# Four normalisation tails reordered: centre and gamma ahead of the root, epsilon as its bias, scale behind it

## The reference

```python
def _layernorm(x, eps=1e-05):
    return (x - mean(x)) / sqrt(var(x) + eps)

h = max(_layernorm(x), 0)                       # layer 0
y = relu((x_sum_of_neighbours(h) + (1 + eps0) * h) @ W1.T + b1) @ W2.T + b2
x = x + ((y - mu(y)) * rsqrt(var(y) + 1e-5) * gamma + beta)

h = max(_layernorm(x), 0)                       # layer 1, attention over the edges, 8 heads
y = h + attention(h) @ Wo
z = (y - mu) * rsqrt(var + 1e-5) * ln1_g + ln1_b
y = z + relu(z @ W1 + b1) @ W2 + b2
x = x + ((y - mu) * rsqrt(var + 1e-5) * ln2_g + ln2_b)

h = max(_layernorm(x), 0)                       # layer 2, edge weights, message width 256
g = relu((messages(h) @ W1 + b1, normalised over 128 features) * gamma + beta)
x = x + where(valid, relu(g @ W2 + b2), 0)

h = max(_layernorm(x), 0)                       # layer 3, mean over neighbours
x = x + relu(mean_of_neighbours(h) @ W_l.T + b_l + h @ W_r.T)
```

## Time and profile before

| | |
|---|---|
| median of three runs | 1396.78 us |
| profiled execution | 1398.88 us |
| its span | 1397.1 us |
| mean granted TensorE clock | 0.948 |
| TensorE busy | 1214.6 us (87%) |
| VectorE busy | 647.5 us (46%) |
| ScalarE busy | 427.1 us (31%) |
| GpSimd busy | 138.5 us (10%) |

### The profile page before, as it was taken

The page is one execution under the profiler, slowest core; times in us unless marked ns, Lnnn a source line. Parts: engine busy times, 40 slices in busy tenths (PEclk is TensorE's granted clock), DMA queues, the critical chain, the costliest instruction groups (busy, mean ns, idle before and its releaser), DMA issues.

```text
span 1397.1 us, 18693 instructions
## 1 busy us (share of the span) xinstructions
PE 1214.6 (87%) x6185; PEld 745.0 (53%) x6185; DVE 647.5 (46%) x1642; ACT 427.1 (31%) x708; POOL 138.5 (10%) x113
## 2 busy tenths in 40 slices
PE   1477777778899998998999999999987999899998
PEld 0244444444465544555777777775446655655543
DVE  6766666666500485003666666665557200540033
ACT  2401122222000434104565555653335301650000
POOL 0000000000145224000000000002326000200000
PEclk9978897878899999999999999999999999999999
DMA  4012344444677610100000000006000032000010
GB/s 138 0 27 56 88 129 137 125 137 132 210 283 249 213 61 30 41 20 1 1 2 1 2 2 1 2 2 247 0 0 31 1 135 79 1 30 0 0 38 36
DMA packets 41609, 93.85 MB, mean 67 GB/s; under 512 B 5113, under 2 KB 9920, under 8 KB 41526
## 3 DMA queue, kind: packets, MB, share of 16 engines
q1 hardware_dynamic: 41526, 92.74, 20.8%
HBM read 51.76 MB, written 34.56 MB: 62 GB/s over the span
## 4 chain that ended last, share of the span: by engine, by line
PE 76%; DVE 11%; issue 6%; ACT 3%; DVEq 2%; DMA 1%; SPq 0%; POOLq 0%; POOL 0%; ACTq 0%
PE PS L403 14%; PE PS L615 6%; PE PS L437 6%; PE PS L598 6%; PE PS L730 6%; PE PS L572 6%; PE PS L479 5%; PE PS L764 5%; PE PS L543 5%; PE PS L701 3%; PE PS L709 3%; PE PS L452 2%; PE PS L533 2%; DVE R L1000 2%; DVE stats L861 2%
## 5 line engine op out<-in xcount | busy, mean ns | idle before, releaser
L403 PE MATMUL PS<-HT,R 125*128 (+1 forms) x988 | 241.7, 379 | 96.9 <-DVE HT L885 43.8
L885 DVE TENSOR_SCALAR HT<-BC,K 125x626 f16 (+1 forms) x494 | 193.0, 443 | 115.1 <-PE PS L403 77.2
L403 PEld LDWEIGHTS PS<-HT,R 125*128 x988 | 139.0, 158 | 199.4 <-issue 177.3
L989 DVE CUSTOM_DVE_ANT_0 HT<-PS,CD 128x1250 f32<-128x1250 f32 (+1 forms) x80 | 116.4, 1454 | 54.2 <-issue 54.2
L1153 ACT COPY HT<-PS 128x626 f32<-128x626 f32 x80 | 54.6, 683 | 253.4 <-PE PS L403 251.2
L598 PE MATMUL PS<-K,HT 128*128 128x128 f32 (+2 forms) x800 | 111.7, 278 | 15.8 <-DVE R L1000 15.0
L1247 ACT ACTIVATE HT<-HT,soft 128x1250 f32<-128x1250 f32 (+1 forms) x80 | 107.1, 1338 | 19.9 <-DVE soft L992 12.6
L598 PEld LDWEIGHTS PS<-K,HT 128*128 128x128 f32 (+2 forms) x800 | 83.4, 140 | 43.5 <-DVE R L1000 24.2
L1227 ACT COPY R<-PS 128x512 f32<-128x512 f32 (+1 forms) x120 | 64.8, 574 | 120.1 <-PE PS L598 118.2
L572 PE MATMUL PS<-R 64*128 64x512 f32 (+3 forms) x480 | 94.8, 526 | 4.8 <-DVE soft L989 3.1
L615 PE MATMUL PS<-R 128*64 128x128 f32 (+2 forms) x1600 | 94.2, 273 | 0.0
(11 more groups left out here) (192 smaller groups left out, 1381.5 us busy)
## 6 DMA issues: line engine op xcount, KB each, us to landing
edge_parts<-HT SPq DMA_DIRECT2D x80, 234.4 KB
X<-edge_parts SPq DMA_DIRECT2D x15, 625.0 KB, 5.7
R<-edge_parts SPq DMA_DIRECT2D x15, 625.0 KB, 5.8
CD<-HT SPq DMA_DIRECT2D x160, 39.1 KB
edge_counts<-CD SPq DMA_DIRECT2D x10, 625.0 KB, 5.9
CD<-edge_sums SPq DMA_DIRECT2D x1, 6250.0 KB, 21.6
CD<-edge_counts SPq DMA_DIRECT2D x1, 6250.0 KB, 17.8
X<-in_x SPq DMA_DIRECT2D x2, 2304.0 KB
```

The lines of the kernel that those rows point to most:

```text
L403: i = mm(bank(b0 + h, PIECE), stat, hot[:, h * PIECE:(h + 1) * PIECE], start=first, stop=True, skip_group_check=True)
L885: return ve.tensor_scalar(slot, iota[0:EC, :], K1[0:EC, K_BASE + w:K_BASE + w + 1], col, ALU.add, ALU.is_equal)
L989: ve.tensor_tensor_reduce(Pb[s][a][0:n], PS[0:n, a * N:(a + 1) * N], cd[0:n, t, :], 1.0, -3e38, ALU.add, ALU.max, soft[0:n, s, a:a + 1]).t ...
```

## The change

In the four tails the order of the normalisation is another. Before: scale and shift on ScalarE, (y x scale - mean x scale), then gamma on VectorE. After: (y - mean) x gamma in one scalar_tensor_tensor on VectorE, right behind the variance and ahead of the root's use; then y x scale on ScalarE, as a Copy with a per-partition scale and no bias. GpSimd's beta addition waits for ScalarE's scaling (`_z`) and no longer for a gamma product (`_zg`). Epsilon is no longer added by VectorE: the root takes it as a per-partition bias from a constant. Since `spread_of` and `root` are shared, that also holds for the three norms of x behind the first tail, the third tail and the loop `l2b`.

```diff
+            ve.memset(gate[:, 1:2], LN_EPS)
 ...
             def spread_of(y, n, slot, name, s, m):
                 link(ve.bn_stats(s[0:n, 0, :], y))
-                link(ve.bn_aggr(m[0:n, slot, :], s[0:n, 0, :]))
-                ve.tensor_scalar(m[0:n, slot, 1:2], m[0:n, slot, 1:2], LN_EPS, None, ALU.add).then_inc(sem(name + "_var"), 1)
+                ve.bn_aggr(m[0:n, slot, :], s[0:n, 0, :]).then_inc(sem(name + "_var"), 1)
 ...
-            def spread_of_y(name, t, w=D, buf=ybuf):
-                spread_of(y_of(t, w, buf), rows(t), t % 4, name, stats, mv)
-            def scale_of_y(name, t):
-                scale_of(rows(t), t % 4, name, t, mv, rs)
-            def scaled(st, t, gamma, w=D, buf=ybuf):
-                n = rows(t)
-                dve.wait_ge(sem(st + "_z"), t + 1)
-                ve.tensor_tensor(y_of(t, w, buf), y_of(t, w, buf), gamma[0:n], ALU.mult).then_inc(sem(st + "_zg"), 1)
+            def spread_of_y(st, t, gamma, w=D, buf=ybuf):
+                n, y = rows(t), y_of(t, w, buf)
+                spread_of(y, n, t % 4, st + "_yn", stats, mv)
+                dve.wait_ge(sem(st + "_yn_var"), t + 1)
+                ve.scalar_tensor_tensor(y, y, mv[0:n, t % 4, 0:1], gamma[0:n], ALU.subtract, ALU.mult)
+            def scale_of_y(st, t):
+                n = rows(t)
+                dve.wait_ge(sem(st + "_yn_std"), t + 1)
+                ve.reciprocal(rs[0:n, t % 4, 0:1], rs[0:n, t % 4, 0:1]).then_inc(sem(st + "_yn"), 1)
 ...
-                    spread_of_y("l0_yn", t)
+                    spread_of_y("l0", t, bc0[:, 1, :])
                 if 1 <= t <= T:
-                    scale_of_y("l0_yn", t - 1)
-                if 2 <= t < T + 2:
-                    scaled("l0", t - 2, bc0[:, 1, :])
+                    scale_of_y("l0", t - 1)
 ...
-                sc.activation(r[0:n, t % 4, 0:1], m[0:n, t % 4, 1:2], ACT.Sqrt).then_inc(sem(name + "_std"), 1)
+                sc.activation(r[0:n, t % 4, 0:1], m[0:n, t % 4, 1:2], ACT.Sqrt, bias=gate[0:n, 1:2]).then_inc(sem(name + "_std"), 1)
 ...
-                sc.activation(buf[0:n, t % 4, 0:w], buf[0:n, t % 4, 0:w], ACT.Identity, bias=rs[0:n, t % 4, 1:2],
-                              scale=rs[0:n, t % 4, 0:1]).then_inc(sem(st + "_z"), 1)
+                sc.activation(buf[0:n, t % 4, 0:w], buf[0:n, t % 4, 0:w], ACT.Copy, scale=rs[0:n, t % 4, 0:1])\
+                    .then_inc(sem(st + "_z"), 1)
 ...
-                    pool.wait_ge(sem(st + "_zg"), t + 1)
+                    pool.wait_ge(sem(st + "_z"), t + 1)
```

More of the change, by code:

```diff
@@ L1014, in _ @@
             dve.wait_ge(sem("l1_bc_in"), 80)
-            for t in range(T + 2):
+            for t in range(T + 1):
                 if t < T:
@@ L1022, in _ @@
                     dve.wait_ge(sem("l1a_y"), t + 1)
-                    spread_of_y("l1a_yn", t, D, ybuf1)
+                    spread_of_y("l1a", t, bc1[:, 0, :], D, ybuf1)
                 if 1 <= t <= T:
-                    scale_of_y("l1a_yn", t - 1)
-                if t >= 2:
-                    scaled("l1a", t - 2, bc1[:, 0, :], D, ybuf1)
+                    scale_of_y("l1a", t - 1)
             for t in range(T + 4):
@@ L1036, in _ @@
                     dve.wait_ge(sem("l1b_y"), t + 1)
-                    spread_of_y("l1b_yn", t, D, ybuf1)
+                    spread_of_y("l1b", t, bc1[:, 2, :], D, ybuf1)
                 if 1 <= t <= T:
-                    scale_of_y("l1b_yn", t - 1)
-                if 2 <= t < T + 2:
-                    scaled("l1b", t - 2, bc1[:, 2, :], D, ybuf1)
+                    scale_of_y("l1b", t - 1)
                 if 3 <= t < T + 3:
@@ L1079, in _ @@
                     dve.wait_ge(sem("l2a_y"), t + 1)
-                    spread_of_y("l2a_yn", t, P, ybuf2)
+                    spread_of_y("l2a", t, g_bc, P, ybuf2)
                 if 1 <= t <= T:
-                    scale_of_y("l2a_yn", t - 1)
-                if t >= 2:
-                    scaled("l2a", t - 2, g_bc, P, ybuf2)
+                    scale_of_y("l2a", t - 1)
             for t in range(T + 1):
@@ L1350, in _ @@
                 n = rows(t)
-                pool.wait_ge(sem("l1a_zg"), t + 1)
+                pool.wait_ge(sem("l1a_z"), t + 1)
                 gp.tensor_tensor(H[0:n, t, :], ybuf1[0:n, t % 4, :], bc1[0:n, 1, :], ALU.add).then_inc(sem("l1_x1"), 1)
@@ L1358, in _ @@
                 n = rows(t)
-                pool.wait_ge(sem("l2a_zg"), t + 1)
+                pool.wait_ge(sem("l2a_z"), t + 1)
                 gp.tensor_tensor(ybuf2[0:n, t % 4, 0:P], ybuf2[0:n, t % 4, 0:P], be_bc[0:n], ALU.add)\
```

## The result

Four runs of the changed kernel gave 1406.55 to 1407.62 us, median 1407.34; four of the kernel before beside them a median of 1395.64. The ratio is 1.0081, interval 1.0057 to 1.0105: slower by 0.8%, beyond the noise. A second set of twelve gave 1.0066 (1.0046 to 1.0085). The forecast was 1402.2 us in 1393.5 to 1406. The sign was right, the size was not, and the time lies above the range. Two single executions far outside the spread, one of 2386.59 us (order alone, experiment 3) and one of 1430.12 us (the kernel before), are left out of every figure here.

A forecast was written before the change was run, and what follows sets the result against it. TensorE bounds the kernel, waiting in the tails on ScalarE's copies behind VectorE, which sets the pace in the first and third. 2.2 + 0.55 + 0.3 + 4.3 - 0.9 - 1.0 = +5.4 us gave 1402.2 us, range 1393.5 to 1406.

The forecast's parts named there:

- The mechanism: First and third tails: VectorE operations with two SBUF tensors wait out GpSimd's whole addition, 1.27 us, if it starts first.
- Period 4.52: VectorE's pass in the first tail: 4.52 us from one add to the next, 0.56 us more than now.
- The margin by which L869 comes too late: L869 of x comes up 0.11 us after GpSimd's beta addition starts, and is held until 0.02 us behind its end.
- First stall: TensorE's 2.47 us wait ahead of the first value product of the first tail: +2.2 us.
- second: TensorE's 1.15 us wait later in the first tail, behind the last tile's add: +0.55 us.
- second tail: The 2.72 us stall ahead of the feed-forward product: scaling comes 0.41 us later, is 0.10 shorter, +0.3 us.
- Third tail: Adds held while the pipeline fills, about 2.0 us, then 0.56 us more each pass: +4.3 us.
- the 3.33 us stall: TensorE's wait ahead of the third tail's fifth turned tile; the copy for it was to come 4.3 us later.
- Fourth: Fourth tail, 128 wide: ScalarE's scaling 0.10 us shorter per tile, -0.9 us for ten tiles.
- The loop behind it: L1090: x's epsilon add goes, -0.18 us per tile, six tiles ahead of the 2.74 us stall, -1.0 us.
- rival 3: A now harmless 1.15 us stall becomes 1.7 us and lets TensorE's clock fall: 1.7 us per case; chance 0.10.
- The base: Start of the forecast time: profiled execution of 1398.9 us lies 2.1 us above the runs' median, 1396.8.

The follow-up runs named there:

- experiment 3: The change's halves, each against the kernel before: new order with epsilon still added by VectorE, 1410.61 us (1.0089); epsilon as root's bias alone, 1394.07 us (0.9964).
- experiment 7: Filler matmuls in TensorE's stalls of the first and second tails: changed kernel 1402.39 us (1.0016), kernel before 1398.03 us (0.9997).
- the late memset: Changed kernel with the epsilon constant's memset moved behind the window loops: ratio 1.0059 to the kernel before, 942.6 us behind L452.
- The kernel before with the memset: Kernel before plus the changed kernel's 128x1 memset at the start, which nothing reads there: ratio 0.9990, 936.1 us behind L452.
- the kernel with narrowed additions: Changed kernel with GpSimd's beta and x additions in the first and third tails on 16 of 512 columns: 1392.06 us, 0.9962.

## Why the prediction missed

*The mechanism held.* Period 4.52, as forecast; L869 1.22 us, ended 0.02 us behind GpSimd's addition; L940 0.75 us, held in the fill; scaling 0.72 us. The margin by which L869 comes too late was 0.06 us and not 0.11. By the page "SBUF — State Buffer" of the Trainium skill, section "SBUF: two separate sides", whoever starts first gets the shared ports for its whole instruction. The traces agree: GpSimd 0.02 us ahead made L869 take 1.26 us; L869 0.10 us ahead of GpSimd took 0.16; and L940 0.18 us ahead of GpSimd made GpSimd's addition 0.43 us longer.

*The terms.* First stall forecast +2.2, measured +1.95; second +0.55, +0.56; second tail +0.3, +0.31 of stall; together, with the clock left out, the first two tails gave +2.9 and +0.3 (experiment 7) for +2.75 and +0.3. Third tail +4.3: the turned tile behind the 3.33 us stall came 4.2 us later, the stage is +3.7 and +4.8 (3.5 with the late memset). Fourth -0.9, -0.9. The loop behind it: -1.0 forecast, -2.6 measured. Its pass fell from 2.00 to 1.79 us, so that five passes ahead of the stall give -1.1; most of the rest is the clock. The kernel before with the memset, alike in this loop, lost less clock there and took 107.56 us instead of 108.45, and where the losses were alike (changed with the late memset, 106.71) the difference is 0.85. So each wait and each saving was sized about right: 2.9 + 0.3 + 4.2 - 0.9 - 1.0 = 5.5, where the sum had 5.4.

*The step that failed is the clock, which the sum put at nothing.* The text had it as a rival at 0.10, 1.7 us for a stall that is harmless now and starts to cost. It took the falls that were there already as constant in size, and so had no term for a longer stall losing more. But the loss behind the first stall went from 1.7 to 2.9 us (6.56 against 3.70, before 5.37) in four executions of five, and the second tail's went from 1.7 to 3.0 in one of two. A fall came in the attention stage too, +1.0 and +0.8 us, though not through a longer stall: the kernel with narrowed additions has it as well, behind a first stall of 0.84 us. Less was lost in the loop behind the fourth tail. Net, the profiled executions lie 6.7 us apart behind L452, 1.3 more than the sum. Experiment 7 shows that such losses are the clock and not the wait: same stalls, TensorE kept busy, 5.8 us back in the profiled execution, 5.0 by the means of all executions (1406.8 to 1401.8), and 0.2 in the kernel before; the difference of the two, 4.8, is known to +-3. That rival 3 named the clock was right; the case it priced, a harmless stall of 1.15 us that starts to cost, did not happen (1.71 us, 3.70 us behind it). The page "VectorE: DVE Perf Modes" of the Trainium skill, section "Rules for kernel authors", advises to minimise the count of operations; the trace does not bear that out here, as the prediction feared: three operations fewer a pass, VectorE's pass 0.56 us longer.

*The base was off too.* I took 2.1 us off because the profiled execution lay above the median of three. 116 executions of the kernel before average 1398.40 us; 23 of the changed one (with the late memset) 1406.8. So: base +1.6, clock in the profiled executions +1.3 (6.7 - 5.4), a part that is not placed +1.7 (8.4 - 6.7), first four runs of the result above their average +0.5: 1402.2 + 5.1 = 1407.3. No one of these alone takes the time out of the range; that they all point the same way is in part bad luck. The range left no room for a clock term, although showed 1.7 us behind one stall.

*What stays open.* Behind L452 the profiled executions differ by 6.7 us, all executions over their whole length by 8.4 +- 1.0. Over the 116 of before the time falls by 4.4 us for each 0.01 of mean clock; the changed kernel's mean clock is 0.9429 against 0.9470, worth 1.8 us. That fits the 1.7 us that are not placed, but it is a correlation: in which stage the executions without a profile lost them isn't known. Nor was it settled why a 2.47 us stall is followed by a fall in one execution and not in the next, or what set the fall in the attention stage.

## What to carry to other kernels

Where VectorE and GpSimd share a saturated loop, lay their operations side by side in time before counting them. In these runs a scalar_tensor_tensor or tensor_tensor with two tensors in SBUF, be it 128x1, lost what was left of GpSimd's instruction if it came hundredths of a microsecond later (1.26 us instead of 0.16), and nothing if it came first. Give the small ones one tensor. Hold a short GpSimd chain back where nobody waits for it.

And price a longer stall of TensorE with the clock behind it, each stall by what its fall already costs, and take the base from as many executions as there are: a stage that comes ahead of the change can vary by more than the change is worth.

## What was not expected of the hardware

- The wait is decided by starts 0.02 us apart (528.78 and 528.80); in that execution it came out the same way in each of the six full passes of the first tail (1.26 us each).
- A fall of the clock removed at one place came back at another in the kernel before (behind the first stall at 528 us, then behind 650), so that filling its stalls gained nothing, while in the changed kernel filling them gained 5.8 us.
- A tensor_scalar whose second tensor is a per-partition scalar (L869, 0.21 us) is not held by GpSimd, a scalar_tensor_tensor with the same two 128x1 operands in SBUF is.
- Where VectorE was ahead, GpSimd's addition to x took 1.70 instead of 1.27 us beside a VectorE operation of 0.75 us that had begun 0.18 us earlier: it lost 0.43 of the 0.57 us that were left of it.
